# Scaling a node block's update by its reciprocal deviation: one VectorE multiplication of four tiles in place of four ScalarE instructions

## The reference

```python
em = jnp.concatenate([x[src], x[dst]], axis=-1)
em = jax.nn.relu(layer_norm(em @ msg_w + msg_b, msg_g, msg_beta))
em = em * edge_weights[:, None]
msgs = jax.ops.segment_sum(em, dst, num_segments=num_nodes)
messages = msgs / (counts + 1e-08) * valid
gate = jax.nn.sigmoid(x @ gate_w + gate_b)
combined = jnp.concatenate([x, messages], axis=-1)
h_new = jax.nn.relu(layer_norm(combined @ upd_w + upd_b, upd_g, upd_beta))
r = gate * h_new + (1.0 - gate) * x
out = _layernorm(x + r)
```

## Time and profile before

| | |
|---|---|
| runs (device us) | 707.39, 704.17, 703.56 |
| median | 704.17 |
| the profiled execution's span | 708.1 |
| TensorE busy, mean granted clock | 594.4 us (84%), 0.969 |
| VectorE busy | 549.4 us (78%) |
| ScalarE busy | 537.9 us (76%) |
| GpSimd busy | 396.5 us (56%) |
| moved by DMA | 118.11 MB |

### The profile page before, as it was taken

The page is one execution under the profiler, slowest core; times in us unless marked ns, Lnnn a source line. Parts: engine busy times, 40 slices in busy tenths (PEclk is TensorE's granted clock), DMA queues, the critical chain, the costliest instruction groups (busy, mean ns, idle before and its releaser), DMA issues.

```text
span 708.1 us, 20411 instructions
## 1 busy us (share of the span) xinstructions
PE 594.4 (84%) x4796; PEld 539.4 (76%) x4796; DVE 549.4 (78%) x2526; ACT 537.9 (76%) x2500; POOL 396.5 (56%) x445
## 2 busy tenths in 40 slices
PE   0456999989999998899899898898899889989772
PEld 0446988878888888788788887887888878879662
DVE  4951477878878788788788787887887878888876
ACT  0022797887888888878879888788798888888863
POOL 1766776666566656666556566575675665650000
PEclk9975999999999999999999999999999999999997
DMA  3225576777676766767667676777676776775632
GB/s 94 59 59 135 139 187 181 190 188 181 177 191 186 184 180 184 188 178 183 183 175 185 182 190 178 185 189 179 184 185 181 191 187 175 192 184 155 164 106 60
DMA packets 199084, 118.11 MB, mean 167 GB/s; under 512 B 15053, under 2 KB 192662, under 8 KB 199062
## 3 DMA queue, kind: packets, MB, share of 16 engines
q1 hardware_dynamic: 184822, 91.76, 47.6%
q0 software_dynamic: 12544, 25.72, 16.1%
q10 hardware_dynamic: 1696, 0.40, 0.2%
HBM read 78.85 MB, written 38.97 MB: 166 GB/s over the span
## 4 chain that ended last, share of the span: by engine, by line
DMA 35%; DVE 24%; issue 14%; SPq 9%; PE 6%; ACT 5%; POOL 4%; DVEq 3%; POOLq 0%; ACTq 0%
DMA rows_scratch<-msg_rows 18%; DMA window<-rows_scratch 15%; DVE out_rows L998 8%; DVE y L953 7%; SPq L364 4%; DVE y_stats L960 4%; POOL pair_rows L466 3%; SPq L366 3%; DVE dst_place L934 1%; DVE msg_rows L929 1%; DMA pair_rows<-in_x,idx_slot 1%; DMA halo_i<-in_dst 1%; PE ps_u L700 1%; PE ps_u L698 1%; ACT squares L539 1%
## 5 line engine op out<-in xcount | busy, mean ns | idle before, releaser
L466 POOL DMA_INDIRECT pair_rows<-in_x,idx_slot x392 | 384.5, 981 | 149.9 <-issue 110.2
L539 ACT ACTIVATE squares<-ps_u 128x128 f32<-128x128 f32 x392 | 103.6, 273 | 66.4 <-PE ps_u L700 66.0
L698 PE MATMUL ps_u<-u_x_gate,xT 128*128 128x129 f32 x784 | 153.0, 277 | 0.0
L700 PE MATMUL ps_u<-window,onehot 128*128 128x128 f32 x784 | 152.6, 277 | 0.0
L953 DVE SCALAR_TENSOR_TENSOR y<-ps_h,gate_small,x_rows 128x128 f32<-128x128 f32 x392 | 110.1, 344 | 18.3 <-PE ps_h L716 17.9
L698 PEld LDWEIGHTS ps_u<-u_x_gate,xT 128*128 128x128 f32 x784 | 120.4, 194 | 1.8
L700 PEld LDWEIGHTS ps_u<-window,onehot 128*128 128x128 f32 x784 | 120.3, 194 | 0.0
L998 DVE TENSOR_SCALAR out_rows<-y,y_small,y_rstd 128x128 f32<-128x128 f32 x392 | 110.1, 352 | 5.7 <-ACT y_rstd L560 5.6
L571 ACT ACTIVATE un<-ps_u,u_rstd 128x128 f32<-128x128 f32 x392 | 111.7, 375 | 0.1
L716 PE MATMUL ps_h<-const_in,hT 128*128 128x128 f32 x392 | 62.4, 282 | 33.6 <-ACT hT L578 33.1
L960 DVE BATCH_NORM_STATS2 y_stats<-y 128x6 f32<-128x128 f32 x392 | 85.5, 281 | 3.3
(11 more groups left out here) (135 smaller groups left out, 1139.1 us busy)
## 6 DMA issues: line engine op xcount, KB each, us to landing
window<-rows_scratch SPq DMA_DIRECT2D x196, 129.0 KB, 2.5
x_rows<-in_x SPq DMA_DIRECT2D x98, 256.0 KB
out<-out_rows SPq DMA_DIRECT2D x98, 256.0 KB
rows_scratch<-msg_rows SPq DMA_DIRECT2D x49, 258.0 KB
pair_rows<-in_x,idx_slot POOLq DMA_INDIRECT x392
const_in<-in_constants SPq DMA_DIRECT2D x1, 845.0 KB, 4.8
rows_scratch<-pad_rows SPq DMA_DIRECT2D x5, 64.5 KB, 2.6
weights<-in_L_gnn_msg_w ACTq DMA_DIRECT2D x1, 128.0 KB, 4.8
```

The source lines that it names most:

```text
L466: nc.gpsimd.indirect_dma_start(rows[s][:, j * P:(j + 1) * P], None, x, bass.IndirectOffsetOnAxis(ap=idx_slot[s][:, j:j + 1], axis=0)).then ...
L539: last = nc.scalar.activation(squares[:, b, j * P:(j + 1) * P], u_tile(j, P), ACT.Square, accum_out=u_square[b][:, j:j + 1])
L698: nc.tensor.matmul(u_tile(j, ROW), tile(xT[b], j), u_x_gate[:], start=False, stop=False, skip_group_check=True)
L700: last = nc.tensor.matmul(u_tile(j, P), tile(onehot[b], j), window[2 * ks + b][:, j * ROW:j * ROW + P], start=False, stop=True, skip_group ...
```

## The change

`u_norm` moves from ScalarE to VectorE. On ScalarE it was four instructions for a block, one for each tile, with a signal after each pair (one PSUM bank each); on VectorE it is one `tensor_tensor` over all four tiles, which reads both banks through a view (`u_values`) and raises the signal by two at its end. It waits for `u_rstd`, for the gate's exponential and for the transposes of the former block. It stands between `result` and `residual` in each half.

```diff
         u_by_bank = ps_u[:].rearrange("p (a c) -> p a c", a=2)[:, :, 0:2 * ROW].rearrange(
             "p a (t h) -> p a t h", h=ROW)
+        u_values = u_by_bank[:, :, :, 0:P]
...
-            def u_norm(q, b, kh, ks):
-                act.wait_ge(u_rstd_ready, q + 1)
-                wait(act, n3_done, q - 1)
-                for a in range(2):
-                    for j in (2 * a, 2 * a + 1):
-                        last = nc.scalar.activation(un[b][:, j * P:(j + 1) * P], u_tile(j, P), ACT.Copy,
-                                                    scale=u_rstd[b][:, j:j + 1])
-                    last.then_inc(un_ready, 1)
-
...
                         on(emT_of, former)
-                        on(u_norm, at[1])
                         on(xT_of, at[0])
...
                         on(xT_of, at[0])
-                        on(u_norm, at[1])
                         on(z_rstd_of, this)
...
+            def u_norm(q, b, kh, ks):
+                dve.wait_ge(u_rstd_ready, q + 1)
+                dve.wait_ge(gate_exp_ready, q + 1)
+                wait(dve, n3_done, q - 1)
+                v.tensor_tensor(un[b][:].rearrange("p (a t h) -> p a t h", a=2, h=P), u_values,
+                                u_rstd[b][:].rearrange("p (a t) -> p a t", a=2).unsqueeze(3).to_broadcast(
+                                    [P, 2, 2, P]), ALU.mult).then_inc(un_ready, 2)
+
...
                     on(result, at[3])
+                    on(u_norm, at[1])
                     on(residual, at[2])
```

## The result

| | before | changed |
|---|---|---|
| median of 5 runs (us) | 704.65 | 726.88 |
| lowest, highest | 703.56, 707.39 | 726.18, 735.91 |
| the profiled execution's span | 708.1 | 734.1 |

The ratio is 1.0341, 95% interval [1.0286, 1.0397]. The profiled execution of the changed kernel was the slowest of its five, some 8 to 10 us above the others, so its trace shows 26.0 us of growth where the medians show 22.2.

The account below looks back on a forecast made before the run. The loop through DRAM, from windows' landing to message-row store and back, was taken as the bound. 29.3 + 0.7 + 0.6 = 30.6 us on 704.2 gave 734.8 us, range 721 to 751.

Parts of the forecast that it names:

- The bound: Main loop carried through DRAM: VectorE work between windows' landing and message-row store is paid every turn, 12.76 us a turn.
- The step of 0.61 us: New VectorE multiplication between result and residual: delays its successor 0.61 us, taken from zn; in the first half this lengthens the turn.
- the far bound of 1.13: Price of the new VectorE instruction if joining the tiles gained nothing: 1.13 us, giving 759.8 us.
- The full duration as the price: New VectorE instruction charged its whole 0.69 us, with nothing overlapped; the sum some 4 us higher.
- ScalarE's relief at nothing: Removing ScalarE's four instructions a block, 111.7 us busy in all, gains zero on the loop.
- The added waits: New VectorE instruction's waits for u_rstd, the gate's exponential and the former block's transposes: all covered, no cost.
- TensorE's banks: VectorE frees the ps_u banks later, so the next update begins about 0.7 us later; covered before y and message_update.
- 48 turns: Main loop: 48 turns x 0.61 us = 29.3 us of growth.
- rival 1: Store and window DMA path gives back 0.3 us a turn, so growth is 16 us, to 720 us; chance 0.11.
- The four turns with a short wait, 0.7 us: Four turns where VectorE waits under 0.61 us for windows: second insertion not all hidden, about 0.7 us together.
- The drain, +0.6: After the last window, the new instruction stands between out_rows and y in the chain: 0.6 us more.
- Rival 3: If the true circle ran through the second half, VectorE's 0.69 replacing ScalarE's 1.13 gains 21 us: 683 us; chance 0.04.

Follow-up runs that it names:

- extra_inside: Kernel before plus one 128x512 VectorE instruction writing an unread buffer, ahead of residual in the first half: 1.0271, 729.9 us.
- extra_outside: Kernel before plus one 128x512 VectorE instruction writing an unread buffer, behind the first half's small sums: 1.0008, 709.9 us.
- act_kept: Changed kernel with four ScalarE instructions a block in the old places, scaling SBUF into a scratch buffer: 1.0469, 743.5 us.
- second_only: Changed kernel with VectorE scaling only in the second half of a turn, ScalarE in the first: 0.9973 of the kernel before.
- first_only: Changed kernel with VectorE scaling only in the first half of a turn, ScalarE in the second: 1.042 of the kernel before, 738.4 us.
- after_again: The changed kernel itself, unaltered, run again in another set of runs: 1.0509 of the kernel before, 747.6 against 712.3 us.

## Why the prediction was right, and where it was not

*The bound.* Right. The wait for windows ended last in 49 turns before and in 49 after, and `extra_inside` against `extra_outside` shows by itself that the place of the work decides and not VectorE's load.

*The step of 0.61 us.* Right: the stretch grew from 4.91 to 5.52. `un` lasts 0.68 us with its two-bank read, and its successor starts 0.60 after it, so the far bound of 1.13 fell. The full duration as the price fell too. I had drawn it from "The DRAIN you can't avoid" in "VectorE: DVE Perf Modes" of the Trainium skill; the same section also says that a next operation starts earlier where nothing holds it, which I had left out, and the trace agrees: 0.60 us against a recorded 0.68.

*ScalarE's relief at nothing.* Right by `act_kept` for the changed kernel. In the second half it shortened VectorE's waits for z, which I had not counted; `second_only` is 0.3% faster, within its interval.

*The added waits.* Right: the new instruction waited once, 1.6 us in all, for `u_rstd`.

*TensorE's banks.* Right: I put `update` 0.7 us later, and the trace has it 2.67 us after `dst_place` (403.87) where it was 1.95. In the second half it is 8.52 after it, where it was 7.75.

```profile
405.23 1.06 PE L670 MATMUL ps_z<-weights,emT 128*128 128x128 f32 x8
406.54 0.28 PE L639 MATMUL ps_u<-upd_bias,ones_bf 128*128 128x258 bf16 x1 [0.25 <-DVE un L925]
...
412.39 0.28 PE L639 MATMUL ps_u<-upd_bias,ones_bf 128*128 128x258 bf16 x1 [0.37 <-DVE un L925]
```

The waits are 0.25 and 0.37 us in the two halves, and the cover held: `y` waited for TensorE once, 0.7 us.

*48 turns.* Right as a count, too high as a product. In the profiled executions the growth is 26.0 us: 0.8 in the head (first waiting `dst_place` at 69.81, 68.99 before), 22.0 in the 44 middle turns, 4.0 in the four others, -0.8 in the drain. A middle turn grew by 0.50 and not by 0.61 (12.86 to 13.36). The rest is in the DMA part: the mean from row store to windows' issue went from 4.61 to 4.55 and from there to `dst_place` from 3.33 to 3.29. That is rival 1 in part, with the sign that I had given for it, the stretch at 5.5 and the DMA part shorter. I had set this term at zero, and it is the term that was mis-sized. By the medians, 22.2 us, a turn grew by about 0.46 if all of it is spread over the turns, which puts the term at half the 0.3 that rival 1 gave; the measured 726.9 lies a little nearer to rival 1's 720 than to my 734.8. In two other sets of runs the growth was 30 and 35 us (`first_only` and `after_again`), with nothing given back, and in the set of `first_only` it was 21 us for `extra_inside`. So no single value would have been right; the range of 721 to 751 covers the result with the bounds of the term and not by knowledge of it.

*The last turn.* My sum had nothing of its own for it. The four turns outside the middle grew by 0.2, -0.3, 1.5 and 2.6 us. In the last one no row store is left, and the chain of the changed kernel runs from the windows through `out_rows` and `un` on VectorE into `update`. TensorE had been idle for 3.46 us before this `update`, which then ran at the lower level of its clock (0.50 granted from 697.9 to 703.0):

```profile
697.27 0.61 DVE un L925
...
698.39 0.43 PE ps_u L688 x2
```

From its start at 698.01 to the squares it took 4.1 us; the next three took 2.2 to 2.4.

*The four turns with a short wait, 0.7 us.* Not seen as such: the second half's insertion took the place of waits for z and for TensorE, and the wait for windows stayed at 1.56 us in the middle turns.

*The drain, +0.6.* Right where I had put it, and covered by TensorE's clock: the whole stretch after the last wait shrank by 0.8 us, from 26.6 to 25.8. The new instruction is in the chain there, as I said,

```profile
720.28 0.86 DVE out_rows L996 x3
721.14 0.60 DVE un L925
```

and from the squares of the last `update` to `y` it takes 3.34 us (718.47 to 721.81) where it took 2.74 (693.03 to 695.77), 0.60 more. The kernel before had ScalarE's `un` in its chain ahead of two updates (682.50 and 689.99), but to replace it gained nothing: these updates start 0.29 us later and 0.01 earlier than before, counted from the last wait and from the squares ahead of them. What shrank is one `update`, 3.82 us from its start at 683.91 to the squares in the kernel before, and 2.21 in the changed one (710.97 to 713.18). The chain of the kernel before has

```profile
682.50 0.88 ACT un L571 x3
...
686.41 0.43 PE ps_u L700 x2
```

and the changed one

```profile
711.24 0.22 PE ps_u L688 x2
```

TensorE had been idle for 0.98 us before the slow one and for 1.28 us before the other; the granted clock was 0.50, the lower level, from 684.2 to 687.5, and 1.00 from 710.9 to 713.0. These 1.61 us are more than the 0.8 by which the drain shrank. The changed kernel paid about as much in its last turn, at 698.01, so the two nearly cancel in the total.

*Rival 3, faster,* had its mechanism on the wrong circle. The rule of the Trainium skill ("ScalarE: Activation LUTs", section "Rules for kernel authors"), multiplications on VectorE and not on ScalarE, holds here for the instructions' own time (111.7 us became 66.8) and not for the kernel's.

Open: why one stretch of 5.5 us costs 21 to 35 us in different kernels and sets of runs, and why `first_only` costs 8.5 us more than `extra_inside` on one chip. In the traces the differences lie between the row store and the next `dst_place`, and no run here varied that path alone in the changed kernel.

## What to carry to other kernels

When every engine has idle time, look for the loop that is carried through memory, and price an instruction by whether it stands between the landing and the store of that loop, not by its engine's load: here 0.6 us were worth 21 us in one place and nothing in the other. Before shortening such a loop, list what stands in the issuing queue ahead of its transfer; here the store of a result that nobody waited for held back the loads that everybody waited for, and moving the one behind the other took the ratio from 0.980 to 0.954 (on two chips, each against the kernel before).

## What the runs showed of the hardware

A VectorE instruction of 128x512 float32 that reads two PSUM banks with a stride of 129 columns and a broadcast second operand took 682 ns on average, as the one-bank form does (688 ns), and let its successor start after 0.60 us.

```profile
L925 DVE TENSOR_TENSOR un<-ps_u,u_rstd 128x512 f32<-128x512 f32 x98 | 66.8, 682 | 1.6 <-ACT u_rstd L565 1.6
```

The same `update` took 2.2 us from its start to the squares at a granted clock of 1.00 (1.2 and 2.4 GHz are its two levels, and this is the higher) and 3.8 us at 0.50.

The cost of the same edit differed between two sets of runs (ratios 1.034 and 1.051, with intervals that don't meet). The second set is from one chip, for the first no chip is named, so it isn't shown that the chip makes the difference.
